# The end of the second expert mixture: the sum of a token's expert rows goes through PSUM, and its normalization to ScalarE

## The reference, cut to what matters

```python
def _L1_ffn_ref(x, ...):                    # E = 32 experts, K = 4 a token
    ...                                     # scores, top 4, weights w, each expert's place for the token
    h = silu(einsum('ecd,edi->eci', xe, W1)) * einsum('ecd,edi->eci', xe, W3)
    ye = einsum('eci,eid->ecd', h, W2)
    yrows = ye[eid, posc] * gflat[:, None]
    out = yrows.reshape(-1, K, D).sum(axis=1)
    out = out + silu(X @ sw1.T) * (X @ sw3.T) @ sw2.T
    return out.reshape(x.shape)

x = _layernorm(x + _L1_ffn_ref(x, ...))     # (x - m) / sqrt(v + eps)
```

## Time and profile before

| | us |
|---|---|
| three runs | 2780.26, 2783.45, 2788.93 |
| median | 2783.45 |
| the profiled execution, whole | 2806.97 |
| its span, first to last instruction or transfer | 2805.2 |
| end part: first load of `yr` issued | 2722.4 |
| end part: VectorE starts its first addition | 2727.35 |
| end part: last normalization done | 2800.4 |

### The profile page before, as it was taken

The page is one execution under the profiler, slowest core; times in us unless marked ns, Lnnn a source line. Parts: engine busy times, 40 slices in busy tenths (PEclk is TensorE's granted clock), DMA queues, the critical chain, the costliest instruction groups (busy, mean ns, idle before and its releaser), DMA issues. The chain is left out here.

```text
span 2805.2 us, 50816 instructions
## 1 busy us (share of the span) xinstructions
PE 2415.6 (86%) x17497; PEld 2030.9 (72%) x17498; DVE 1924.5 (69%) x5156; ACT 1120.9 (40%) x2057; POOL 1030.4 (37%) x1419
## 2 busy tenths in 40 slices
PE   3999997999999599999999999978888888884870
PEld 3878885566665499999999999977765666653860
DVE  6999992566766466667766667648674777774558
ACT  2665563455555222222122122213654555542650
POOL 3554552111111164317715425111121344535664
PEclk8999999999999799999999999989998999986885
DMA  3343101333220210012212112014003334210535
GB/s 98 99 149 118 39 1 33 78 80 111 69 80 25 83 38 30 30 68 69 72 34 71 64 35 73 29 33 150 1 14 97 95 85 125 70 40 3 154 131 235
DMA packets 163950, 203.95 MB, mean 73 GB/s; under 512 B 21027, under 2 KB 138062, under 8 KB 163792
## 3 DMA queue, kind: packets, MB, share of 16 engines
q1 hardware_dynamic: 132704, 152.04, 18.3%
q10 hardware_dynamic: 15440, 26.22, 2.6%
q0 software_dynamic: 15648, 23.70, 2.5%
HBM read 95.49 MB, written 75.45 MB: 61 GB/s over the span
## 5 line engine op out<-in xcount | busy, mean ns | idle before, releaser
L1666 PE MATMUL m_gu<-m_x_hi,m_w_hi 128*128 128x256 f32 x1632 | 461.9, 283 | 17.9 <-issue 10.5
L1666 PE MATMUL m_gu<-m_x_hi,m_w_lo 128*128 128x256 f32 x1632 | 457.4, 280 | 0.0
L1666 PE MATMUL m_gu<-m_x_lo,m_w_hi 128*128 128x256 f32 x1632 | 457.4, 280 | 0.0
L1703 ACT ACTIVATE m_sg<-m_gu 128x256 f32<-128x256 f32 x408 | 157.0, 385 | 665.8 <-PE m_gu L1666 646.2
L1172 ACT ACTIVATE x_pt<-x_ps 128x1024 f32<-128x1024 f32 x256 | 262.2, 1024 | 228.4 <-PE x_ps L984 203.6
L1739 DVE TENSOR_TENSOR m_h<-m_sg,m_gu 128x256 f32<-128x256 f32 x408 | 171.4, 420 | 255.6 <-ACT m_sg L1703 248.8
L1666 PEld LDWEIGHTS m_gu<-m_x_hi,m_w_hi 128*128 128x128 f32 x1632 | 310.7, 190 | 21.7 <-issue 11.9
L1666 PEld LDWEIGHTS m_gu<-m_x_lo,m_w_hi 128*128 128x128 f32 x1632 | 309.2, 189 | 0.0
L1666 PEld LDWEIGHTS m_gu<-m_x_hi,m_w_lo 128*128 128x128 f32 x1632 | 308.5, 189 | 0.0
L1277 DVE CUSTOM_DVE_ANT_0 x_ps<-x_ps,x_mb 128x256 f32<-128x256 f32 x512 | 201.4, 455 | 115.6 <-PE x_ps L984 115.5
L1655 PE MATMUL m_yp<-m_w_hi,m_h_hi 128*128 128x256 f32 x816 | 238.5, 292 | 6.4 <-DVE m_h_lo L1741 6.3
(11 more groups left out here) (326 smaller groups left out, 5640.4 us busy)
## 6 DMA issues: line engine op xcount, KB each, us to landing
yt<-zero SPq DMA_DIRECT2D x8, 2048.0 KB, 10.7
x_kpack<-x_kh SPq DMA_DIRECT2D x128, 128.0 KB, 3.1
x_qpack<-x_qh SPq DMA_DIRECT2D x128, 128.0 KB, 3.0
m_yr<-yt SPq DMA_DIRECT2D x16, 1024.0 KB, 13.6
m_x<-xs SPq DMA_DIRECT2D x36, 258.0 KB
xs<-zero SPq DMA_DIRECT2D x8, 1072.0 KB, 6.0
m_x<-xs SPq DMA_DIRECT2D x32, 268.0 KB
c_cx<-in_ctx SPq DMA_DIRECT2D x32, 256.0 KB, 3.1
```

Source lines behind the costliest of these rows:

```text
L1666: ins = pe.matmul(gu[:, m % 4, n, :], wp[n][:, c, m * P:m * P + P], xp_[:, c, :], start=(c == 0 and k == 0), stop=(c == KC - 1 and k == 2))
L1703: act.activation(sg[:, m % 4, :], gu[:, m % 4, 0, :], ACT.Silu).then_inc(silu_ready, 1)
```

## The change

All of it is in `moe1_stage`, behind the last tile. VectorE keeps the first addition alone (`halve`, rows 0 and 1 plus rows 2 and 3) and the statistics, which it now reads from PSUM (`spread`, `average`). TensorE forms the sum in a PSUM bank for each slot: `keep(s)` multiplies the slot of `st.res` (512 columns) by the identity with `start=True`, and `sum_up(s)` multiplies the two halves of `yr` by the identity into the same bank, `start=False`. The first eight `keep` come ahead of the loads, the other eight each behind the sum four slots before, once the slot that had the bank has been normalized. GpSimd forms 1/std and -mean/std (`rstd`, `shift`) for two slots at a time, and one at a time for the last two. ScalarE normalizes out of PSUM into `st.res` with `Identity(scale * x + bias)` and issues the store of slot s - 1 behind the normalization of slot s. `pool_rstd`, `dve_stats` and `dve_normalize` are no longer called here.

```diff
-        TURN, GATE, DOWN = 0, 2, 4
+        TURN, GATE, DOWN, SUM = 0, 2, 4, 6
+        AHEAD = 5
+        GROUPS = [(s, s + 1) for s in range(0, B - 2, 2)] + [(B - 2,), (B - 1,)]
+        GROUP_OF = {s: g for g, group in enumerate(GROUPS) for s in group}
...
+        def sums(s):
+            return bank((SUM + s) % W)
...
-            for s in range(B):
-                pool_rstd(pool, st, var, rstd, s % W, varr, rstdr, epsr, s + 1)
+            def rstd_of(g):
...
+                pool.wait_ge(varr, last + 1)
+                if last >= W:
+                    pool.wait_ge(xn_ready, last - W + 1)
+                pool.tensor_tensor(rstd[:, u, :], var[:, u, :, 1], eps, ALU.add).then_inc(epsr, 1)
+                pool.tensor_tensor(shift[:, u, :], zero, var[:, u, :, 0], ALU.subtract).then_inc(epsr, 1)
+                pool.wait_ge(epsr, 2 * g + 2)
+                pool.tensor_tensor(rstd[:, u, :], rstd[:, u, :], neghalf, ALU.pow).then_inc(rootr, 1)
+                pool.wait_ge(rootr, g + 1)
+                pool.tensor_tensor(shift[:, u, :], shift[:, u, :], rstd[:, u, :], ALU.mult).then_inc(rstdr, 1)
...
+            def keep(s):
+                pe.matmul(sums(s), st.ident[:], st.res[:, blocks(s), :], start=True, stop=False)
+
+            def sum_up(s):
+                pe.wait_ge(halved, s + 1)
+                for j in range(2):
+                    ins = pe.matmul(sums(s), st.ident[:], yr[:, s % W, :, j, :], start=False, stop=(j == 1))
+                ins.then_inc(summed, 1)
+
+            pe.wait_ge(added, B)
+            for s in range(W):
+                if s == W - U:
+                    pe.wait_ge(y_ready, E1)
+                keep(s)
+            for s in range(B):
+                sum_up(s)
+                if AHEAD <= s + 1 < B - W + AHEAD:
+                    pe.wait_ge(xn_ready, s + 2 - AHEAD)
+                    keep(s + 1 + W - AHEAD)
...
-            for s in range(B):
+            def normalize(s):
+                act.wait_ge(rstdr, GROUP_OF[s] + 1)
+                for t in range(TB):
+                    ins = act.activation(st.res[:, TB * s + t, :], sums(s)[:, t, :], ACT.Identity,
+                                         bias=shift[:, s % W, t:t + 1], scale=rstd[:, s % W, t:t + 1])
+                ins.then_inc(xn_ready, 1)
+
+            def store(s):
                 act.wait_ge(xn_ready, s + 1)
                 act.dma_start(out_v[:, blocks(s), :], st.res[:, blocks(s), :]).then_inc(stored, 16)
+
+            for s in range(B):
+                normalize(s)
+                if s:
+                    store(s - 1)
+            store(B - 1)
...
-            def sum_up(i):
+            def halve(i):
                 u = i % W
                 dve.wait_ge(yr_loaded[u], 16 * (i // W + 1))
-                s.do(dve.tensor_tensor(yr[:, u, :, 0:2, :], yr[:, u, :, 0:2, :], yr[:, u, :, 2:4, :], ALU.add))
-                s.do(dve.tensor_tensor(yr[:, u, :, 0, :], yr[:, u, :, 0, :], yr[:, u, :, 1, :], ALU.add))
-                n_sum = s.mark(dve.tensor_tensor(st.res[:, blocks(i), :], st.res[:, blocks(i), :], yr[:, u, :, 0, :], ALU.add))
-                s.after(n_sum)
-                dve.sem_inc(summed, 1)
-                dve_stats(dve, st, s, st.res[:, blocks(i), :], stats, var, u, varr)
-
-            def normalize(i):
-                dve.wait_ge(rstdr, i + 1)
-                dve_normalize(dve, st.res[:, blocks(i), :], st.res[:, blocks(i), :], var, rstd, i % W).then_inc(xn_ready, 1)
+                dve.tensor_tensor(yr[:, u, :, 0:2, :], yr[:, u, :, 0:2, :], yr[:, u, :, 2:4, :], ALU.add).then_inc(halved, 1)
+
+            def spread(i):
+                dve.wait_ge(summed, i + 1)
+                for t in range(TB):
+                    n = s.mark(dve.bn_stats(stats[:, i % W, t, :], sums(i)[:, t, :]))
+                return n
+
+            def average(i, n):
+                u = i % W
+                s.after(n)
+                if i >= W:
+                    dve.wait_ge(rstdr, GROUP_OF[i - W] + 1)
+                dve.bn_aggr(var[:, u, 0, :], stats[:, u, 0, :])
+                dve.bn_aggr(var[:, u, 1, :], stats[:, u, 1, :]).then_inc(varr, 1)
...
+            for i in range(U):
+                halve(i)
             for i in range(B):
-                sum_up(i)
-                if i:
-                    normalize(i - 1)
-            normalize(B - 1)
+                n = spread(i)
+                if i + U < B:
+                    halve(i + U)
+                average(i, n)
```

More of the change, by code:

```diff
@@ L2109, in moe1_stage @@
         var = sb("var", [P, W, TB, 2])
-        rstd = sb("rstd", [P, W, TB])
+        rstd, shift = sb("rstd", [P, W, TB]), sb("shift", [P, W, TB])
         ps = ctx.enter_context(nc.psum_tensor("m1_ps", [P, 8, 512], F32))
-        TURN, GATE, DOWN = 0, 2, 4
+        TURN, GATE, DOWN, SUM = 0, 2, 4, 6
+        AHEAD = 5
+        GROUPS = [(s, s + 1) for s in range(0, B - 2, 2)] + [(B - 2,), (B - 1,)]
+        GROUP_OF = {s: g for g, group in enumerate(GROUPS) for s in group}
         def bank(n):
@@ L2125, in moe1_stage @@
         y_ready, added, dest_ready = sem("y_ready"), sem("shared_added"), sem("dest_ready")
-        summed, stored = sem("rows_summed"), sem("stored")
+        halved, summed, stored = sem("rows_halved"), sem("rows_summed"), sem("stored")
         steps = sem("dve_steps")
         varr, rstdr, epsr, xn_ready = sem("var_ready"), sem("rstd_ready"), sem("eps_added"), sem("xn_ready")
+        rootr = sem("root_ready")
         block = ctx.enter_context(nc.Block())
@@ L2193, in _ @@
                 send(r)
-            for s in range(B):
-                pool_rstd(pool, st, var, rstd, s % W, varr, rstdr, epsr, s + 1)
+            def rstd_of(g):
+                first, last = GROUPS[g][0], GROUPS[g][-1]
+                u = slice(first % W, last % W + 1)
+                eps, neghalf, zero = (c[:, 0:TB * len(GROUPS[g])].rearrange("p (s t) -> p s t", t=TB)
+                                      for c in (st.eps, st.neghalf, st.zero))
+                pool.wait_ge(varr, last + 1)
[7 more added lines that the diff above has]
+                pool.tensor_tensor(shift[:, u, :], shift[:, u, :], rstd[:, u, :], ALU.mult).then_inc(rstdr, 1)
+            for g in range(len(GROUPS)):
+                rstd_of(g)
         @block.tensor
```

## The result

The changed kernel takes 2762.42 us (median of five, 2758.49 to 2769.92) against 2783.45: ratio 0.9931, 95% interval 0.9917 to 0.9946. The forecast was 2764. In its profiled execution the span is 2760.7 us. The profiled execution of before was 23.5 us slower than the median of its runs. So I compare the **end part**, from the first load's issue to the end of the span: 82.8 us before (2805.2 - 2722.4), 60.5 after (2760.7 - 2700.2), 22.3 less. The forecast was 63.1 (2785.5 - 2722.4).

What follows compares the result with a forecast made beforehand. VectorE bound at 4.50 us a slot, the transfers next. Last load at 2772.0, the last slot's chain to 2784.4 and 1.1 for the clock gave span 2785.5, 19.7 us less: median about 2764 us, range 2758 to 2772.

Steps and rivals of the forecast that it cites:

- The bound of before and the bound after: End part: VectorE bounds before at 4.50 us a slot; after, the transfers, 2.56 us a load, 3.2 with a store.
- Sum 2.3 us, with pickups 2.6 us a slot: VectorE's remaining work per slot: halve 1.24, two statistics 0.77, two aggregations 0.25; below the transfers' 2.56 to 3.2 us.
- The rival of an expensive product: TensorE's 512-column product with strided input costs more than 0.86 us and its double; at 2.1 us median 2801; chance 0.04.
- The clock: TensorE starts the sums at 1.2 GHz, reaches 2.4 within two or three slots, perhaps low again in slots 12 to 15.
- The rival with 1.2 GHz all the way: TensorE's 40 products at 1.72 us take 69 us; span 2807, median 2785, no change; chance 0.07.
- the prediction's hard form of it: TensorE: by the skill's rule, waits for DMA make every slot run cold, giving the time of the 1.2 GHz rival.
- The 1.1 us that I added for a low clock in slots 12 to 15: Term in the end sum for TensorE's clock in the last slots, where a low clock costs 1.7 us for two products.
- The kernel in which the clock swings: Rival: TensorE's products average 1.29 us, 40 take 52 us; span 2790, median 2768; counted with a gain, chance 0.12.
- DMA: Loads never starve; two to three more stores among them cost 1.3 to 1.9 us, last load seen at 2772.0.
- GpSimd and ScalarE: Neither bounds: GpSimd 1.7 to 2.8 us of 5.6 per slot pair, ScalarE 1.5 us a slot.
- The sum: From last load at 2772.0 through the last slot's chain to 2784.4, plus 1.1 for the clock: span 2785.5.
- my sign of 12 to 14 us behind the last landed load: Expected in the profile after: the span ends 12 to 14 us behind the last landed load.

## Why the prediction was right, point by point

*The bound of before and the bound after.* Right, up to the last load. VectorE's 4.50 us a slot were the pace, the transfers lay just under it, and the change goes down to them; the half loads and the held stores move the end, while the order of VectorE's aggregation and TensorE's start don't.

*VectorE.* The step "Sum 2.3 us, with pickups 2.6 us a slot" was too high: 2.03 in the run with half the loads. The instructions overlap at their ends (in that run the statistics that start at 2732.55 and take 0.76 us end behind the next halving's start, 2733.23). It changed nothing in the sum, but it made me name the wrong next bound for that run: it is TensorE's three products, 2.58 us.

*TensorE.* The product of 512 columns costs 0.86 us, as taken from two with 256, and the input in pieces costs nothing more. The rival of an expensive product is refuted by this row and by four products a slot, 4.29 us for five.

*The clock.* It was low at the start and rose while TensorE was busy throughout, within three slots; a start at the high clock brought nothing. The rival with 1.2 GHz all the way is refuted: the waits of 1.1 us between the last slots did not bring the clock down, the trace has 1.00. The Trainium skill's warning, TensorE: Matmul & The Clock Gate, section "Loop structure matters more than you think", is of a long wait for DMA between matmuls. The trace agrees for the gap of 6.0 us ahead of the first sums, behind which it has 0.50; the prediction's hard form of it, in which every wait counts, is not what the page says. The 1.1 us that I added for a low clock in slots 12 to 15 were not needed. The kernel in which the clock swings wasn't seen either.

*DMA.* Right in kind, somewhat high in size. The last halving starts 49.1 us after the first issue, predicted 49.6 (2772.0 - 2722.4). By the traces the last load lands 48.15 us after the first issue before and 49.07 after, 0.9 later instead of 1.5, and up to its last packet 2.47 MB of stores have been moved instead of 2.08 MB: 1.5 stores more, where I had counted two to three. That stores take the loads' capacity is shown by the held ones: 0.44 to 0.56 us for each of five, and 3.9 to 4.5 us for the 9.4 of the change.

*GpSimd and ScalarE.* Neither holds up VectorE or TensorE, as predicted; no such wait is in the list. Four steps took 1.40 us in the last slot (2753.80 to 2755.20), predicted 1.7. At the end, GpSimd is in the path and ScalarE is not, which I had the other way round.

*The sum.* Behind the last halving's start 11.4 us instead of 12.4: from there to the statistics 3.30, predicted 3.26; statistics to aggregation 0.80 instead of 0.90; from there to GpSimd's end 1.78 (2753.42 to 2755.20) instead of 1.95; and from GpSimd's end to the end of the span 5.54 instead of 6.3. This last term is near for a wrong reason. I had put ScalarE's normalization (1.1), a store's issue (0.4) and the 4.8 us that stand in the trace of before behind its last normalization one after the other. In both kernels that time belongs to GpSimd's `DRAIN`, which starts with GpSimd's last step; the last normalization and the last store run beside it and are through 1.8 us earlier after the change (2758.7 against 2760.5). So ScalarE's last step adds nothing to the span, and it is luck that the 4.8 us, read from before, had most of the `DRAIN` in them. It also puts the end outside my sign of 12 to 14 us behind the last landed load. With 0.5 at the loads, 1.0 here and 1.1 of the clock, 63.1 becomes 60.5. In the time the forecast of 19.7 less stands beside 21.0 less.

## What to carry to other kernels

Two bounds can lie close under each other: before moving work off the engine that is in every link of the chain, work out when its inputs have all arrived, since the gain ends there and everything moved after that is free or wasted. Here one half of the change (two additions to TensorE) brought 21.2 of 22.3 us, and ScalarE's half on top of it the last 1.1; the products ahead of need are worth 0.5, the order of the aggregation nothing. When the bound is the transfers, the transfers of the results count too; holding them back only trades the end of the loads against a burst behind them, 345 GB/s instead of 411 here, and what remains is the chain of the last piece. Ask of that chain which engine finishes the program: here it is GpSimd, 5.54 us behind its last arithmetic, and the last normalization and store lie under it. And compare stretches with the same code around them, not spans: the profiled executions differed by 22 us in code that was not touched.

## What the runs showed of the hardware that was not expected

TensorE kept 2.4 GHz through the last slots, busy 2.01 of 3.40 us in the stretch from 2746.3, where I had expected it to fall as it had after the stretch with 1.89 of 3.40. GpSimd's closing `DRAIN` ends 5.3 us behind GpSimd's last arithmetic in all thirteen profiles and sets the end of the span in eleven of them; in the two with the stores last, the burst is longer. The same 256 KB stores move at 345 GB/s by themselves, with the DMA engines full, while loads and stores together reach 411. The causes of these two were not tried.
